# A graph kernel's edge counting: compares for several groups at once, sums behind the first group of a pair, and the diagonal on another engine

## The reference

```python
e = leaky_relu((h @ a_src[l])[src] + (h @ a_dst[l])[dst], SLOPE)
p = exp(e - segment_max(e, dst)[dst])
z = segment_sum((p / segment_sum(p, dst)[dst])[:, None] * h[src], dst) + b[l]
```

## Time and profile before

| | us |
|---|---|
| median of the three runs | 2692.47 |
| the profiled execution, its own time | 2694.59 |
| its span in the trace | 2692.7 |
| the counting stage, first `lo` compare to the next stage's first weight load | 58.07 to 473.41 |
| VectorE busy over the span | 2132.5 |
| ScalarE busy over the span | 1870.0 |
| TensorE busy over the span (matmuls) | 2124.6 |
| GpSimd busy over the span | 86.2 |

### The profile page before, as it was taken

The page is one execution under the profiler, slowest core; times in us unless marked ns, Lnnn a source line. Parts: engine busy times, 40 slices in busy tenths (PEclk is TensorE's granted clock), DMA queues, the critical chain, the costliest instruction groups (busy, mean ns, idle before and its releaser), DMA issues. The chain is left out here.

```text
span 2692.7 us, 90541 instructions
## 1 busy us (share of the span) xinstructions
PE 2124.6 (79%) x34148; PEld 1877.5 (70%) x34148; DVE 2132.5 (79%) x4334; ACT 1870.0 (69%) x3038; POOL 86.2 (3%) x137
## 2 busy tenths in 40 slices
PE   3999997599599598495976899579995899848736
PEld 3655554598498598494866899478894899838724
DVE  7999997688788788615159999889997999967963
ACT  5999997666766766301039999599995999837522
POOL 1111111000000000000000000000000000000000
PEclk8999999799799799698988999789997999969868
DMA  4355455342242342171722332223312333025200
GB/s 101 152 222 210 195 215 221 112 144 78 96 149 85 98 154 78 61 244 50 236 81 89 96 106 61 80 85 95 103 52 82 101 109 96 28 74 159 73 0 25
DMA packets 182326, 302.60 MB, mean 112 GB/s; under 512 B 6476, under 2 KB 158927, under 8 KB 182058
## 3 DMA queue, kind: packets, MB, share of 16 engines
q1 hardware_dynamic: 181273, 297.57, 33.6%
q0 software_dynamic: 800, 1.26, 0.2%
HBM read 214.26 MB, written 84.54 MB: 111 GB/s over the span
## 5 line engine op out<-in xcount | busy, mean ns | idle before, releaser
L438 ACT ACTIVATE stage<-ps 125x375 f32 x625 | 314.1, 604 | 38.0 <-PE ps L384 33.8
L339 DVE TENSOR_SCALAR col<-iota_col,window_col 125x376 bf16<-125x376 f16 x1250 | 310.2, 319 | 3.5 <-PE ps L384 3.5
L384 PE MATMUL ps<-col,lo 125*125 125x375 bf16 x1250 | 289.9, 344 | 17.7 <-DVE col L339 17.4
L1007 ACT ACTIVATE r1amsk<-r1ad,r1thr 125x640 f16 x360 | 260.1, 817 | 3.7 <-DVE r1asel L1029 3.5
L1007 ACT ACTIVATE r2amsk<-r2ad,r2thr 125x640 f16 x360 | 259.6, 816 | 0.1
L1007 ACT ACTIVATE r0amsk<-r0ad,r0thr 125x640 f16 x360 | 259.6, 815 | 0.1
L1080 PE MATMUL ps<-r1mv,r1asel 125*128 125x66 f16 x5000 | 244.0, 196 | 10.7 <-issue 9.4
L1080 PE MATMUL ps<-r2mv,r2asel 125*128 125x66 f16 x5000 | 241.1, 195 | 5.7 <-issue 5.1
L1080 PE MATMUL ps<-r0mv,r0asel 125*128 125x66 f16 x5000 | 244.0, 196 | 0.3 <-DVE r0asel L1029 0.3
L1080 PEld LDWEIGHTS ps<-r1mv,r1asel 125*128 125x128 f16 x5000 | 227.3, 100 | 14.9 <-issue 10.0
L384 PEld LDWEIGHTS ps<-col,lo 125*125 125x125 bf16 x1250 | 136.6, 139 | 144.3 <-DVE col L339 141.5
(11 more groups left out here) (540 smaller groups left out, 4478.9 us busy)
## 6 DMA issues: line engine op xcount, KB each, us to landing
counts<-stage SPq DMA_DIRECT2D x75, 800.0 KB, 4.8
ct<-counts_all SPq DMA_DIRECT2D x75, 800.0 KB, 4.6
counts_all<-total SPq DMA_DIRECT2D x25, 800.0 KB, 7.3
g0ct<-counts_all SPq DMA_DIRECT2D x25, 800.0 KB, 4.6
g1ct<-counts_all SPq DMA_DIRECT2D x25, 800.0 KB, 4.6
g2ct<-counts_all SPq DMA_DIRECT2D x25, 800.0 KB, 4.6
r0ct<-counts SPq DMA_DIRECT2D x25, 800.0 KB, 4.7
r1ct<-counts SPq DMA_DIRECT2D x25, 800.0 KB, 4.9
```

The source lines that it names most:

```text
L339: ins = v.tensor_scalar(col1[:, b % OHS * WIN + w], K.iota_col[:], K.window_col[:, bass.ds(i * (P // DG) + b, 1), w], None, ALU.is_equal)
L384: ins = pe.matmul(K.ps[0:P, s, 0:GW], lo1[:, b, 0:P, w], col1[:, s * WIN + w, 0:GW], start=(w == 0), stop=(w == WIN - 1))
L438: act.activation(dst.rearrange("p a r h d -> p (a r h) d"), K.ps[0:P, b % OHS, 0:GW].rearrange("p (x d) -> p x d", d=DG), ACT.Copy).then_i ...
L1007: act.activation(msk[:, s % 5, n], ad[:, bass.ds(g % 2, 1), h] .rearrange("p a (b d) -> p (a b) d", d=PAD), ACT.Sigmoid, bias=T.thr[:, 1, ...
```

## The change

All of it is in the counting stage, with three buffers resized for it.

- `window_col` becomes a 2-byte float and `iota_pair` 376 pairs long. The `col` compares become two-input compares like those of `lo`: for each five groups one for two groups (1504 elements) and one for three (2256). The one-hots of the two windows lie side by side in pairs, so a matmul reads its moving operand in steps of two elements. `col1` holds three sets of five groups, so VectorE may be five to ten groups ahead.
- TensorE writes group pairs into bank pairs (0,1), (2,3), (4,5), the 25th group alone into bank 2; sums go to banks 6 and 7. A bank is asked for once a pair.
- ScalarE copies a pair with one instruction when both its groups are counted, 12 pairs and one single a block.
- Add-ups stand behind groups 2, 8, 12, 18 and 22, each the first of its pair; the moves follow pairs 1, 4, 6, 9 and 11 on ScalarE.
- Weights, outputs and copies have 128 columns or partitions in place of 125.
- GpSimd has no part in the stage. VectorE adds the diagonal of the block before, in two instructions, behind the third unit of five groups.

The diff, without the branch that this input doesn't use and without the closing waits that are unchanged:

```diff
@@ prepare
-        pi = sb("pi", [P, PAD, 2], I32)
+        pi = sb("pi", [P, GE, 2], I32)
-                pool.iota(pi[:], [[1, PAD], [0, 2]], channel_multiplier=0).then_inc(iotas, 1)
+                pool.iota(pi[:], [[1, GE], [0, 2]], channel_multiplier=0).then_inc(iotas, 1)
@@ count_edges
-    ADDED = (3, 8, 13, 18, 23)
+    ADDED = (2, 8, 12, 18, 22)
+    GROUPS = P // DG
+    SUMS = 6
+    PAIRS = [(b, min(b + 2, GROUPS)) for b in range(0, GROUPS, 2)]
+    BANK = [2 * (p % 3) for p in range(12)] + [2]
+    MOVED = {1: 0, 4: 1, 6: 2, 9: 3, 11: 4}
+    LAST = [max(p for p in range(len(PAIRS)) if BANK[p] == bank) for bank in (0, 2, 4)]
-        col1 = sb("col1", [P, SLOTS, GE], BF16)
+        col1 = sb("col1", [P, 30, GE], BF16)
+        col2 = col1[:].rearrange("p s c -> p (s c)").rearrange("p (a s c w) -> p a s c w", a=3, s=OHS, w=WIN)
-            @block.gpsimd
-            def _(pool):
-                with pool.Fori(0, NB) as i:
-                    pool.wait_ge(moved, 5 * i + 7)
-                    for own in [stage[0:P, bass.ds(i % STAGES, 1), r, bass.ds(i, 1), 0:P] for r in range(R)] + \
-                            [total[0:P, bass.ds(i % 2, 1), bass.ds(i, 1), 0:P]]:
-                        own = own.rearrange("p a h d -> p (a h) d")
-                        pool.tensor_tensor(own, own, K.ident16[0:P, 0:P].unsqueeze(1), ALU.add).then_inc(diag, 1)
             @block.vector
             def _(v):
+                def diagonal(i, slot, other):
+                    v.wait_ge(moved, 5 * i + 7)
+                    for own in (stage[0:P, bass.ds(slot, 1), :, bass.ds(i, 1), 0:P].rearrange("p a r h d -> p (a r h) d"),
+                                total[0:P, bass.ds(other, 1), bass.ds(i, 1), 0:P].rearrange("p a h d -> p (a h) d")):
+                        v.tensor_tensor(own, own, K.ident16[0:P, 0:P].unsqueeze(1).to_broadcast(list(own.shape)),
+                                        ALU.add).then_inc(diag, 1)
+                def one_hots(i, first=False):
+                    for n in range(GROUPS // OHS):
+                        v.wait_ge(counted, i * GROUPS + (5, 10, 10, 15, 20)[n])
+                        v.tensor_tensor(
+                            lo1[:, OHS * n:OHS * n + OHS], K.iota_pair[:, 0:PAD].unsqueeze(1).to_broadcast([P, OHS, PAD, WIN]),
+                            K.window_lo[:, bass.ds(i * GROUPS + OHS * n, OHS)].unsqueeze(2)
+                            .to_broadcast([P, OHS, PAD, WIN]), ALU.is_equal)
+                        for s0, s1 in ((0, 2), (2, OHS)):
+                            v.tensor_tensor(
+                                col2[:, n % 3, s0:s1], K.iota_pair[:].unsqueeze(1).to_broadcast([P, s1 - s0, GE, WIN]),
+                                K.window_col[:, bass.ds(i * GROUPS + OHS * n + s0, s1 - s0)].unsqueeze(2)
+                                .to_broadcast([P, s1 - s0, GE, WIN]), ALU.is_equal).then_inc(hot, s1 - s0)
+                        if n == 2 and not first:
+                            diagonal(i - 1, (i + STAGES - 1) % STAGES, (i + 1) % 2)
...
+                    one_hots(0, True)
+                    with v.Fori(1, NB) as i:
+                        one_hots(i)
...
+                diagonal(NB - 1, (NB - 1) % STAGES, (NB - 1) % 2)
             @block.tensor
-                pe.sem_inc(counted, OHS)
+                pe.sem_inc(counted, 2 * OHS)
                 pe.sem_inc(moved, 1)
+                def bank_free(i, b):
+                    p = b // 2
+                    earlier = [q for q in range(p) if BANK[q] == BANK[p]]
+                    if earlier:
+                        pe.wait_ge(taken, i * GROUPS + PAIRS[earlier[-1]][1] + GROUPS)
+                    else:
+                        pe.wait_ge(taken, i * GROUPS + PAIRS[LAST[BANK[p] // 2]][1])
                 def add_up(i, n, own=True):
-                    pe.wait_ge(taken, i * (P // DG) + 5 * n + OHS)
+                    pe.wait_ge(taken, i * GROUPS + 5 * n + GROUPS)
                     pe.wait_ge(moved, 5 * i + n + 1)
...
-                            pe.wait_ge(hot, i * (P // DG) + b + 1)
-                            pe.wait_ge(taken, i * (P // DG) + b + 1)
+                            pe.wait_ge(hot, i * GROUPS + b + 1)
+                            if b % 2 == 0:
+                                bank_free(i, b)
                             for w in range(WIN):
-                                ins = pe.matmul(K.ps[0:P, s, 0:GW], lo1[:, b, 0:P, w], col1[:, s * WIN + w, 0:GW],
+                                ins = pe.matmul(K.ps[:, BANK[b // 2] + b % 2, 0:GW], lo1[:, b, :, w],
+                                                col2[:, b // OHS % 3, b % OHS, 0:GW, w],
                                                 start=(w == 0), stop=(w == WIN - 1))
                             ins.then_inc(counted, 1)
             @block.scalar
-                act.sem_inc(taken, OHS)
+                act.sem_inc(taken, GROUPS)
...
-                    for b in range(P // DG):
-                        act.wait_ge(counted, i * (P // DG) + b + 1 + OHS)
-                        dst = stage[0:P, bass.ds(i % STAGES, 1), :, :, DG * b:DG * (b + 1)]
-                        act.activation(dst.rearrange("p a r h d -> p (a r h) d"),
-                                       K.ps[0:P, b % OHS, 0:GW].rearrange("p (x d) -> p x d", d=DG),
-                                       ACT.Copy).then_inc(taken, 1)
-                        if b - 1 in ADDED:
-                            move_total(i, ADDED.index(b - 1))
+                    for p, (b0, b1) in enumerate(PAIRS):
+                        act.wait_ge(counted, i * GROUPS + b1 + 2 * OHS)
+                        dst = stage[:, bass.ds(i % STAGES, 1), :, :, DG * b0:DG * b1]
+                        act.activation(dst.rearrange("p a r h (s d) -> p s (a r h) d", d=DG),
+                                       K.ps[:, BANK[p]:BANK[p] + b1 - b0, 0:GW].rearrange("p s (x d) -> p s x d", d=DG),
+                                       ACT.Copy).then_inc(taken, b1 - b0)
+                        if p in MOVED:
+                            move_total(i, MOVED[p])
             @block.sync
-                    sp.wait_ge(diag, 4 * i + 4)
+                    sp.wait_ge(diag, 2 * i + 2)
@@ build
-                K.iota_pair = sb2("iota_pair", [P, PAD, WIN], F16)
+                K.iota_pair = sb2("iota_pair", [P, GE, WIN], F16)
-                K.window_col = sb2("window_col", [P, NG, WIN], F32)
+                K.window_col = sb2("window_col", [P, NG, WIN], F16)
```

More of the change, by code:

```diff
@@ new lines, in wide_one_hots @@
+                def wide_one_hots(i, s):
+                    with v.Fori(0, STEPS) as c:
+                        v.wait_ge(wide_used, i * (OHS * STEPS) + s * STEPS + c + 1)
+                        base = K.group_base[:, bass.ds(i * OHS + s, 1)]
+                        for w in range(SLOTS):
+                            v.tensor_scalar(lo_wide[:, w], K.iota_col[:, 0:PAD],
+                                            K.keys[:, bass.ds(c * SLOTS + w, 1), 0], None, ALU.is_equal)
+                            ins = v.tensor_scalar(col1[:, w], K.iota_col[:], base,
+                                                  K.keys[:, bass.ds(c * SLOTS + w, 1), 1],
+                                                  ALU.add, ALU.is_equal)
+                        ins.then_inc(wide_hot, 1)
@@ L343, in _ @@
-                with v.Else():
[L344 to L356, removed]
+                    one_hots(0, True)
@@ new lines, in _ @@
+                    with v.Fori(1, NB) as i:
+                        one_hots(i)
+                with v.Else():
+                    for b in range(GROUPS):
+                        wide_one_hots(b // OHS, b % OHS)
+                    with v.Fori(1, NB) as i:
+                        for b in range(GROUPS):
+                            if b == 5:
+                                diagonal(i - 1, (i + STAGES - 1) % STAGES, (i + 1) % 2)
+                            wide_one_hots(i * OHS + b // OHS, b % OHS)
@@ L407, in _, with one_group @@
[L407 to L412 removed]
+                    def one_group(i, b):
+                        bank = BANK[b // 2] + b % 2
+                        bank_free(i, b)
+                        pe.matmul(K.ps[:, bank, :], K.zeros[0:P, 0:128], K.zeros[0:P], start=True, stop=True)
+                        with pe.Fori(0, STEPS) as c:
+                            pe.wait_ge(wide_hot, i * (GROUPS * STEPS) + b * STEPS + c + 1)
+                            for w in range(SLOTS):
+                                ins = pe.matmul(K.ps[:, bank, 0:GW], lo_wide[:, w], col1[:, w, 0:GW],
+                                                start=False, stop=False, skip_group_check=True)
+                            ins.then_inc(wide_used, 1)
+                        pe.matmul(K.ps[:, bank, 0:128], K.zeros[0:P, 0:128], K.zeros[0:P, 0:128], start=False, stop=False,
+                                  skip_group_check=True).then_inc(counted, 1)
@@ L414, in _ @@
```

(5 more changed lines are left out.)

41 lines of the change are left out of this document (5 added, 36 removed).

## The result

The changed kernel takes 2753.24 us in the median of four runs, the kernel before 2692.6 beside it: slower, ratio 1.0217, 95% interval 1.0204 to 1.0231. One of the four runs (3091.47) is disturbed and stays out of the ratio; the other three are 2748.46, 2748.92 and 2757.56, so their median is 2748.92. The forecast was 2755, range 2715 to 2790. The profiled execution took 2748.92, its span is 2747.1.

The account below looks back on a forecast made before the run. VectorE bound the kernel before at 15.7 us a block; after, the TensorE-ScalarE path would, at 18.4. 25 x (18.4 - 15.7) = +67.5, less 3.4 and 1.05, gives +63: 2755 us from 2692.47, range 2715 to 2790.

Parts of the forecast that it names:

- The links: Counting stage: five stretches of a block's path to and fro between TensorE and ScalarE, summing to 18.57 us.
- add-ups 2 and 4: Links to the add-ups behind groups 12 and 22, which wait for the move before: 3.23 us each.
- add-ups 1 and 3: Links to the add-ups behind groups 8 and 18, which wait for the pair after the move: 4.09 us each.
- the seam: Link between blocks: the next block's groups 2 and 3 need bank 2, which group 24 used: 3.93 us.
- 128 columns, -0.2: TensorE's loads: 128 columns shorten the one load right after a wait, five a block: -0.2 us a block.
- The end terms: Stage ends: ScalarE's landing wait in the third block goes, -3.4 us; a shorter diagonal after the last move, -1.05.
- VectorE stays the bound: Rival, counting stage: the links don't bind, a block is 14.6 us, the kernel 2660 us; chance 0.08.
- The stepped moving operand at half speed: Rival, group matmuls: reading `col2` in steps halves their speed; a block 21 us, the kernel 2820 us; chance 0.06.
- one sign that I had named for being wrong: Group matmuls on TensorE above 0.16 us from start to start in a row would show the prediction wrong.
- The clock falls: Rival, TensorE: pauses drop its granted clock to 1.2 GHz, up to +160 us, 2915 us; chance 0.03.
- The two-input compares don't run at 0.503 ns: Rival, VectorE: at twice that time an element, a block takes 23 us, +180 us; chance 0.01.
- The 0.81 and 0.72: ScalarE's pair copy by the skill's rule: 0.81 us long, 0.72 start to start; block about 17.4 us, kernel 2730.

Follow-up runs that it names:

- experiment 1: The changed kernel with the add-ups behind the second group of a pair (3, 9, 13, 19, 23), nothing else: 2644.07 us, ratio 0.9805 to the kernel before.
- experiment 7: The changed kernel with 125 columns and partitions in place of 128 in weights, outputs, copies and moves: 2755.65 us, ratio 1.0242.
- experiment 6: The changed kernel with the old one-input col compares and a densely read moving operand: 2750.99 us, ratio 1.0221.
- the version whose links are loose: The version of experiment 1, measured again with nothing altered: 2645.0 us.
- experiment 9: The version of experiment 1 with the old one-input col compares and a densely read moving operand: 2668.59 us, ratio 0.9909.
- (10): The version of experiment 1 with ScalarE copying group by group in place of pairs: 2646.06 us, ratio 0.9828.
- experiment 5: The version of experiment 1 with the diagonal back on GpSimd: 2787.04 us, ratio 1.0363.
- (4): The kernel before with only the diagonal moved from GpSimd to VectorE: 2674.81 us, ratio 0.9917.

## Why the prediction was right, and where it was off

**The mechanism** is shown. The links, forecast and measured: add-ups 2 and 4, 3.23 each and 3.23 and 3.20; add-ups 1 and 3, 4.09 each and 4.25 and 4.24; the seam 3.93 and 3.91. Moving the add-ups by one group takes all of it away (experiment 1).

**The mis-sized terms of the block, 18.4 for 18.83.** The step "add-ups 1 and 3 ... 4.09" is short by 0.15, twice. The link from 204.13 measures 0.86 (to the next group), 0.62 (to the pair), 0.89 (to the move), 0.62 (to the next pair) and 1.26. The first three come to 2.37 where I had 0.89 + 0.48 + 0.96 = 2.33; the last is 1.26 where I had 1.00 + 0.14. The 0.14 was the hand-over from a move to an add-up, and I used it behind a pair as well. Behind a pair it is 0.23 to 0.29. And "128 columns, -0.2" was taken off links that the slow reading of `col2` lengthens: the columns give 0.17 (experiment 7), the stepped reading takes 0.12 (experiment 6), for which I took nothing. With both taken out the links would sum to 18.88 for my 18.57; the wait behind a pair, 0.12 too short in two links, is most of that. The bound of twice the time was far off; the weights' rows pointed the right way but hid a small cost.

**The stage.** Forecast +63; measured +75.6: 25 blocks at 0.43 us more are 11 of the 12.6 missing. The end terms held: the landing wait of 3.38 is gone, and behind the last move VectorE's diagonal takes 0.50 us for GpSimd's 1.55. The first compare is 2.07 us later, a cost that I had at nothing. In the twelve profiled executions with the longer ramp it starts at 58.5 to 60.3, 59.5 in the mean, and in the two with the short ramp at 58.1 and 58.3: scatter, but some 1 us of cost too, of which the longer cast (0.55 us for 0.29) is a part.

**What I didn't see.** That GpSimd, freed of the diagonal, would start the first all-reduce in time: -5.7, readable before in GpSimd's 9.91 idle us. And the -15 in later layers. So that the forecast of 2755 came within 6 us of the undisturbed runs' 2748.92 is in part luck: +12.6 in the stage and -21 behind it nearly cancelled. Without the -21 the kernel would have taken some 2770, still inside the range; the sum was not as good as its result.

**The rivals.** "VectorE stays the bound" fell, and became the timing of experiment 1. "The stepped moving operand at half speed" fell: 0.166 us, not 0.318. But one sign that I had named for being wrong did show, group matmuls more than 0.16 us apart; it told of the small cost above and not of a wrong path. "The clock falls" fell: 1.00 throughout, though TensorE paused five times a block. "The two-input compares don't run at 0.503 ns" fell: 935 and 1326 ns.

**Rule and rows.** The rows' 1.00 us for a pair held (1.02, and 0.87 from start to start, 207.12 to 207.99 in the trace). The 0.81 and 0.72 worked out from the Trainium skill ("ScalarE: Activation LUTs", "What ACT_TABLE_LOAD costs") did not: this trace disagrees with it. The block and the time that I gave for them don't follow either: seven pairs of 0.81 in place of 1.00 make 17.1 us and 2722, not 17.4 and 2730. By the section on "cachelines" of "SBUF — State Buffer" in the Trainium skill stepped reading would be free; it costs 4 per cent of a matmul.

**What each part is worth**, in the version whose links are loose (2645): two-input compares 23.6 us (experiment 9); pairs 1, which is nothing (10); the diagonal on VectorE 142 with these compares (5), most of it the seven stops behind the long additions, and some 20 by itself in the kernel before (4). The place of the add-ups costs 106 (2751.38, one run, against 2645.0 beside it) and hid the rest.

## What to carry to other kernels

When an engine's work is merged (a pair in place of two copies), look at what the other engines do between the parts: work of another kind that stands between the first and the second part is now in front of both, and if it waits for the merged result in turn, both engines idle and neither is full. Put it behind the whole; here five numbers were worth 106 us. Before merging, write the circle link by link from the trace of before; it came out within 0.16 us of each link.

## What the runs showed of the hardware

- Seven of GpSimd's additions of 125 x 125 (0.42 us) were held for 22 us each by VectorE's back-to-back two-input compares, which lost nothing; all seven began in the last 0.19 us of a compare. Those that began with 0.35 us or more of it left took turns with the compares: 0.6 to 1.5 us each (the first 2.98), the compares 0.23 us longer.
- Beside one-input compares GpSimd's additions to `stage` took 0.44 us in the median and 2.39 at most, and VectorE was the slower for it (473 for 307 ns an instruction).
- A PARTITION_ALL_REDUCE began 9.91 and 9.58 us after the instruction before it when GpSimd had done additions in the stage (the kernel before, experiment 5), and at once on its data when it had not.
- A moving operand of 2-byte elements read in steps of two: 0.166 us a matmul of 375 columns, 0.159 densely. Output of 125 or 128 columns made no difference to it, but the load fell from 137 to 97 ns.
- TensorE's matmuls that waited for ScalarE's copy of a pair (750 elements, 1.02 us) started 0.23 to 0.29 us after its end; those that waited for a move, 0.14 us after.
